# Attention's TensorE order in a fused pre-norm layer: score banks paired with halves of the row maxima, whole value products, and moved work at the edges of the stages

## The reference, cut to what matters

```python
x = L0_attn_x                                  # (4, 2048, 256), float32
x = x + attn(layernorm(x))                     # 16 heads of 16, causal
x = x + ffn(layernorm(x))

# attn:
qkv = x @ W_attn + b_attn
scores = einsum('bhqd,bhkd->bhqk', q, k) * 0.25
probs = softmax(where(causal, scores, -inf))
out = einsum('bhqk,bhkd->bhqd', probs, v) @ W_proj + b_proj

# ffn: ternary weights with one scale per row, a rank-16 term, squared ReLU
h = x @ (tern(w_fc) * scale).T + gate * (x @ v.T @ fast_b.T @ u.T)
y = (max(h, 0) ** 2) @ (tern(w_proj) * scale).T
```

## Time and profile before

| | |
|---|---|
| median of 3 runs | 2120.4 us (2115.23 to 2132.78) |
| profiled execution, its own time | 2129.81 us |
| its span, first to last instruction | 2128.1 us |
| QKV, span time | 0 to 189 us |
| opening, maxima alone | 189 to 237 us |
| attention's 16 units | 237 to 1724 us |
| MLP, first to last matmul | 1746 us to the end |
| PE busy | 2032.3 us, 96% |
| DVE busy | 1850.8 us, 87% |
| ACT busy | 1487.4 us, 70% |
| granted PE clock, mean | 0.967 |

### The profile page before, as it was taken

How to read it: one execution, slowest core, us unless ns; L and a number is a source line. 1 busy time by engine, 2 the same in 40 slices (tenths; PEclk the granted TensorE clock), 3 DMA queues, 4 the chain that set the end, 5 groups by cost and what they waited for, 6 DMA issues and landing times. The chain is left out here.

```text
span 2128.1 us, 46470 instructions
## 1 busy us (share of the span) xinstructions
PE 2032.3 (96%) x18173; PEld 1123.1 (53%) x18173; DVE 1850.8 (87%) x3143; ACT 1487.4 (70%) x2787; POOL 474.8 (22%) x637
## 2 busy tenths in 40 slices
PE   6987899999999999999999999999999969999998
PEld 5875344444444444444444444444444438888887
DVE  7987889999999999999999999999999438998996
ACT  2331378888888888888888888888888535555554
POOL 0000011011110111111011110111111127776774
PEclk9997599999999999999999999999999779999999
DMA  5995121221222212122121211212122122333220
GB/s 192 325 317 215 29 54 47 53 57 38 75 52 60 55 40 65 48 70 47 53 60 34 82 51 54 57 37 71 50 63 62 36 65 80 101 89 90 80 80 30
DMA packets 163003, 168.29 MB, mean 79 GB/s; under 512 B 74704, under 2 KB 102880, under 8 KB 162784
## 3 DMA queue, kind: packets, MB, share of 16 engines
q1 hardware_dynamic: 154112, 157.72, 25.4%
q10 hardware_dynamic: 8672, 7.60, 1.3%
HBM read 95.77 MB, written 67.63 MB: 77 GB/s over the span
## 5 line engine op out<-in xcount | busy, mean ns | idle before, releaser
L984 ACT ACTIVATE probs<-ps_s 128x512 f32<-128x512 f32 x2176 | 1179.3, 596 | 257.8 <-PE ps_s L1177 231.8
L1010 DVE TENSOR_REDUCE maxes<-ps_m 128x2 f32<-128x1024 f32 (+1 forms) x960 | 1141.9, 1220 | 110.5 <-PE ps_m L1140 88.4
L1198 PE MATMUL ps_acc<-probs,vs 128*32 128x256 f32 (+1 forms) x8696 | 703.9, 396 | 11.9 <-ACT acc_sb L962 11.9
L1177 PE MATMUL ps_s<-qs,ks 50*128 50x512 f32 (+3 forms) x2560 | 577.8, 450 | 1.0 <-ACT probs L984 0.9
L1140 PE MATMUL ps_m<-ks,qs 48*128 48x512 f32 (+3 forms) x2560 | 504.4, 392 | 18.7 <-DVE maxes L1010 9.5
L1177 PEld LDWEIGHTS ps_s<-qs,ks 50*128 50x128 f32 x2560 | 255.9, 186 | 414.0 <-ACT probs L984 381.1
L1198 PEld LDWEIGHTS ps_acc<-probs,vs 128*32 128x32 f32 x8696 | 173.7, 108 | 295.1 <-issue 194.7
L918 POOL TENSOR_SCALAR_AFFINE_SELECT probs<-probs 128x512 f32<-128x512 f32 x256 | 160.0, 640 | 744.1 <-ACT probs L984 740.5
L1140 PEld LDWEIGHTS ps_m<-ks,qs 48*128 48x128 f32 x2560 | 265.1, 192 | 94.5 <-DVE maxes L1010 70.7
L1017 DVE CUSTOM_DVE_ANT_0 sums_masked<-ps_m,mask 128x384 f32<-128x384 f32 (+1 forms) x512 | 186.6, 421 | 20.2 <-PE ps_m L1140 4.1
L1382 POOL TENSOR_TENSOR hid<-square,hid 128x512 fp32r<-128x512 f32 x128 | 175.3, 1378 | 107.3 <-DVE square L1393 91.9
(11 more groups left out here) (129 smaller groups left out, 1764.5 us busy)
## 6 DMA issues: line engine op xcount, KB each, us to landing
qs<-q_scr SPq DMA_DIRECT2D x384, 64.0 KB, 2.7
ks<-k_scr SPq DMA_DIRECT2D x384, 64.0 KB, 2.8
q_scr<-probs SPq DMA_DIRECT2D x32, 512.0 KB, 4.0
k_scr<-probs SPq DMA_DIRECT2D x32, 512.0 KB, 5.3
o_scr<-acc_sb SPq DMA_DIRECT2D x64, 256.0 KB, 2.9
v_scr<-probs SPq DMA_DIRECT2D x16, 512.0 KB, 5.8
v_dense<-v_scr SPq DMA_DIRECT2D x16, 512.0 KB, 4.5
o_in<-o_scr SPq DMA_DIRECT2D x32, 256.0 KB
```

The source lines that it names most:

```text
L984: act.activation(probs[:, s % RING, x], ps_s[:, k % BANKS], ACT.Exp).then_inc(ring_taken, 1)
L1010: last = dve.tensor_reduce(maxes[c % 2][:, :, pairs, tt, i], banks, AX.X, ALU.max)
L1177: last = pe.matmul(ps_s[:, k % BANKS, at:at + width], ks[u][rows, j // TT, p, j % TT * P:(j % TT + 1) * P], qs[u][rows, c, p, q0:q0 + widt ...
L1198: last = pe.matmul(ps_acc[h * VW:(h + 1) * VW, q0:q0 + width], vs[u][:, j, h], probs[:, s % RING, h % banks_of(s), at:at + width], start=( ...
```

## The change

In each step the order becomes bank 2i (r = 0), the r = 1 half of an item ("beside"), bank 2i+1 (r = 1), the r = 0 half of the item, for both pairs of banks, and then all value products of the step whole, 512 queries wide. The ring stays at three banks and the maxima at two slots.

At the edges: `fill` issues matmuls whose result nobody reads, behind each of the last ten items of the opening (3), in place of the values in the first three steps (4), and in six steps of the last unit (2). QKV's fixed loads go from ACT's to SP's queue, its first products stand ahead of the second transposes, and its last chunk is stored in the attention block. In the last unit PE's steps for the weights and the projection come earlier, chunk 1's attention output is loaded and scaled there, and the square root is taken ahead of the last copy of the accumulator. What the last accumulator still needs (store_acc, invert_sums, store_recip) moves into the MLP block, and ACT's high part of chunk 1 behind that of chunk 0.

```diff
 def order(s, last):
     x = sum(banks_of(i) // 2 for i in range(s))
-    if banks_of(s) == 4:
-        got = [("bank", 0), ("bank", 1), *items_at(x), ("values", (0,)), ("bank", 2), ("bank", 3), *items_at(x + 1), ("values", (1,))]
-    else:
-        got = [("bank", 0), ("bank", 1), ("values", (0, 1)), *items_at(x)]
+    got = []
+    for i in range(banks_of(s) // 2):
+        item, *others = items_at(x + i)
+        got += [("bank", 2 * i), ("beside", item[1]), ("bank", 2 * i + 1), item, *others]
+    got.append(("values", None))
...
-LOADS_AT, TERNARY_AT, O_AT, X_AT = 5, 16, 19, 22
-LOW_AT, G_AT, W1_AT, W2_AT, S_AT, PROJECT_AT = 17, 22, 25, 29, 33, 34
-SCALE_AT, BIAS_AT, O_HIGH_AT = 26, 30, 33
+LOADS_AT, TERNARY_AT, O_AT, X_AT, O1_AT = 5, 16, 20, 24, 32
+LOW_AT, G_AT, W1_AT, W2_AT, S_AT, PROJECT_AT = 16, 20, 21, 25, 29, 31
+SCALE_AT, BIAS_AT, O_HIGH_AT = 25, 29, 29
+FILLED_ITEMS, FILLED_STEPS = 10, (17, 18, 19, 32, 33, 34)
...
+def fill(pe, w_o, bank, count):
+    for _ in range(count):
+        pe.matmul(bank, w_o[:, 0, 0, 0:P], w_o[:, 0].rearrange("p k d -> p (k d)"), start=True, stop=True, skip_group_check=True)
...
@@ build_qkv, SP @@
+            sp.wait_ge(masked, 3)
...
+            sp.wait_ge(sh.ones_set, 1)
+            load_ones(sp, sh, sh.ks)
...
             def body(n, used, u, left):
+                if left > 0:
+                    store_chunk(sp, scr, sh, n)
@@ build_qkv, PE @@
-                if left >= 1:
+                if left >= 1 and n > 0:
                     transposes(n + 1, 1 - u)
...
                     last.then_inc(qk_ready, 1)
+                if n == 0:
+                    transposes(1, 1)
@@ build_attention, SP @@
+            store_chunk(sp, scr, sh, BATCH * NCH - 1)
...
-                if last:
-                    store_acc(n, NCH - 1)
-                    store_recip(n, NCH - 1)
+                    if last and s == O1_AT:
+                        sp.wait_ge(late.w2_ready, KH // 2)
+                        load_o(sp, scr, lead.o_in[1], lead.r_in[1], lead.o_loaded[1], 1)
@@ build_attention, ACT @@
                 if last:
+                    lead.norm.take_root(act, 0)
                     copy_acc(n, NCH - 1)
-                    lead.norm.take_root(act, 0)
@@ build_attention, PE @@
-            def form_max(n, par, k):
+            def form_max(n, par, k, r):
...
-                if not (isinstance(n, int) and NM * n + k < SLOTS):
+                if r == 1 and NM * n + k >= SLOTS:
                     pe.wait_ge(slot_freed, NM * n + k - SLOTS + 1)
...
-                last.then_inc(slot_filled, 1)
+                if r == 0:
+                    last.then_inc(slot_filled, 1)
...
                 if what == "item":
-                    form_max(0, 0, x[1])
+                    form_max(0, 0, x[1], 1)
+                    form_max(0, 0, x[1], 0)
+                    if x[1] >= LEAD - FILLED_ITEMS:
+                        fill(pe, keep["w_o"], ps_acc[:], 3)
...
+                        elif what in ("beside", "item"):
+                            form_max(*unit_of(x, n, u), 1 if what == "beside" else 0)
...
+                        elif what == "values":
+                            fill(pe, keep["w_o"], ps_acc[:], 4)
+                    if last and s in FILLED_STEPS:
+                        fill(pe, keep["w_o"], ps_m[:, 3], 2)
@@ build_mlp, SP, POOL, ACT @@
-            load(1)
+            load_x(sp, io, x[1], x_loaded[1], 1)
+            store_acc(sp, scr, lead, UNITS - 1, NCH - 1)
...
-            scale(1)
             bias(1)
...
-            act.wait_ge(o_ready, 2)
-            copy_high(act, o_t, o_in[1], o_scaled, o_copied, KD)
             for n in range(CHUNKS):
                 copy_high(act, xn_t, ps_t, turned, turned_copied, KD * n)
+                if n == 0:
+                    act.wait_ge(o_ready, 2)
+                    copy_high(act, o_t, o_in[1], o_scaled, o_copied, KD)
```

More of the change, by code:

```diff
@@ L125, in order @@
     x = sum(banks_of(i) // 2 for i in range(s))
-    if banks_of(s) == 4:
-        got = [("bank", 0), ("bank", 1), *items_at(x), ("values", (0,)), ("bank", 2), ("bank", 3), *items_at(x + 1), ("values", (1,))]
-    else:
-        got = [("bank", 0), ("bank", 1), ("values", (0, 1)), *items_at(x)]
[L130 to L139, removed]
+    got = []
[3 more added lines that the diff above has]
+    got.append(("values", None))
+    return [(what, y) for what, y in got if not (last and what in ("beside", "item", "found", "rows") and y[0])]
 def ring_uses(s, last):
@@ L656, in _ @@
             copy_high(act, xn_t[0], ps_t, xt_ready, xt_copied, 0)
-            act.wait_ge(masked, 3)
-            for r in range(2):
-                for half in range(2):
-                    for dst, src in ((sh.ident_half, keep["ident_h"]), (sh.mask_half, keep["mask_h"])):
-                        act.dma_start(dst[ROW * r:ROW * (r + 1), half], src[ROW * half:ROW * (half + 1), :]).then_inc(sh.fixed_in, 16)
-            act.wait_ge(sh.ones_set, 1)
-            load_ones(act, sh, sh.ks)
             norm.take_root(act, 1)
@@ L1115, in body @@
                         take_w2()
+                    if last and s == PROJECT_AT:
+                        copy_low(dve, lead.o_t, lead.o_in[0], lead.o_copied, lead.o_split, 0)
+                        for i in range(2):
+                            residual(dve, lead, lead.x, lead.x1, 0, i)
+                        lead.norm.variance(dve, 0)
                 if last:
-                    copy_low(dve, lead.o_t, lead.o_in, lead.o_copied, lead.o_split, 0)
-                    for i in range(2):
-                        residual(dve, lead, lead.x, lead.x1, 0, i)
-                    lead.norm.variance(dve, 0)
                     lead.norm.normalise(dve, lead.x1, lead.xn, 0).then_inc(lead.xn_ready, 1)
-                    invert(n, NCH - 1)
             over_units(dve, body)
@@ L1199, in values @@
                                          probs[:, s % RING, h % banks_of(s), at:at + width],
-                                         start=(j == 0 and 0 in halves), stop=(s + 1 in CHUNK_END), skip_group_check=True)
-                if 1 in halves:
-                    last.then_inc(pv_done, 1)
+                                         start=(j == 0), stop=(s + 1 in CHUNK_END), skip_group_check=True)
+                last.then_inc(pv_done, 1)
             def turn_low(n):
@@ L1237, in turn_scales @@
             def turn_scales():
+                pe.wait_ge(late.rows_made, 1)
                 pe.wait_ge(late.w2_taken, 3)
```

167 lines of the change are left out of this document (89 added, 78 removed).

## The result

The changed kernel took a median of 2195.9 us (2188.9 to 2198.6, four runs), the kernel before 2126.6 us (2115.2 to 2136.1, four runs) on the same chip: 1.032 times the time (95% interval 1.028 to 1.036). The forecast of 2138 had the sign right and the size wrong by 58 us, and the result lies outside the stated range of 2085 to 2168.

The account below looks back on a forecast made before the run. PE was taken to bound most of the kernel, with the bank ring's limit hidden behind it. Full steps +50, last unit -1, opening -8.5, QKV -6, way to MLP -18: +17 on 2120.4 gave 2138 us, range 2085 to 2168.

Parts of the forecast that it names:

- Part 1, full steps: Attention steps: a full step goes from 2.47 to 2.58 us; +3.3 a unit, +50 for 15 units.
- The ring: Three score banks: bank 3 waits for bank 0's exp, a loop of 1.24 us where three slots give only 1.0.
- a slot of 0.34: Full steps: the values follow bank 3's start by 0.34 us, in the sum 1.24 + 0.34 + 1.00 = 2.58.
- the slots: Steps with masked items in a row: an item's first half waits for its maxima slot; 0.5 us a unit, bounded by 1.2.
- Part 2, last unit: Last unit of attention: longer steps and fills against a held clock, sum -1 us (-4 to +11).
- the fills and the denser work would hold the clock: Last unit: TensorE's clock stays at 1.00 in steps with form_w1 and step 24, giving 11 us back.
- the clock falls in attention: Rival: waits in each step drop the clock to 0.50, costing 28 us per 85 us stretch; 2166 us, chance 0.10.
- Part 3, opening: Opening and first unit: fills raise the clock early; -8.5 us (-11 to +9).
- three items: Opening: the clock stays at 0.50 for only three items with fills, costing +2.5 us.
- the fills don't do what they are for: Rival: clock stays 0.50 through the opening and falls in the last unit; 2149 to 2165 us, chance 0.18.
- Part 4, QKV: QKV block: earlier end without the last chunk's store and earlier first products; -6 us (-9 to -2).
- Part 5: Attention to MLP: a copy's wait goes (-14), the root moves ahead, PE keeps its clock (3 less); -18 us (-20 to -13).

Follow-up runs that it names:

- kernel 3: Changed kernel with the new pairs kept but the values cut in halves, one behind each pair of banks; 2103.8 us, ratio 0.990.
- experiment 4: Changed kernel with both heads of an item together behind each pair of banks, values whole at the end; 2279.7 us, one execution.
- kernel 5: Changed kernel with exps over 256 of 512 columns in all units but the first; 2106.2 us, one execution.
- kernel 10: Changed kernel with exps over 64 of 512 columns in all units but the first and reductions over half the keys; 2005.3 us, one execution.
- kernel 6: Changed kernel with plain reductions over half of each item's keys; 2160.2 us, one execution.
- kernel 9: kernel 3 with one opening burst of sixteen fills, and chunk 1's x loaded and its bias added in the last unit; 2102.1 us, ratio 0.992.
- kernel 11: kernel 9 without the twelve fills of the last unit; 2100.1 us, ratio 0.991.
- kernel 7: kernel 3 without any fills in the opening and the first unit; 2103.4 us, ratio 0.991.
- kernel 12: Changed kernel with the old step order and halved values, exps over 64 columns except in the first unit, half-length reductions; 2089.7 us, one execution.

## Why the prediction was wrong

**Part 1, full steps: right mechanism, undersized.** The ring, its loop of 1.24 and the direction stood in the forecast and in the trace, and experiments 3, 4 and 5 show them from three sides. For the fifteen units I said +50; it was 59.8 for fourteen, and one more at 4.27 makes 64. Two terms were too small. I read the starts of the first exps of each step and took medians over the steady units, before and after:

```
steps of a unit                                       before    after   sum of differences   forecast
22 full steps, of which 19 at 2.66 to 2.68 after   2.46-2.72  2.66-2.80      +3.2              +2.35
5 steps where masked items stand in a row          2.79-2.99  3.16-3.50      +1.9              +1.05
5 others of four banks (two plain, three short)    2.43-2.67  2.39-2.73      -0.3              -0.1
4 steps of two banks                               1.67-2.07  1.59-1.88      -0.5               0
```

The first term is the stretch from bank 3 to the values. This is the step of the sum that failed: the prediction took a slot of 0.34; it is 0.43 after the wait, in kernel 10 without a long wait too, and 0.32 in kernel 3, where the values follow the second pair. I think of the weights of the values, whose load lies open there; no run separates it. The 0.09 on a full step is the difference between 2.58 and 2.67. The second is the slots: not 0.5 but up to 1.9 a unit, of which kernel 6 removes only 0.8 (in two of the five steps). What holds the other three, 17, 24 and 27 of a unit counted from 0, with half-length reductions as well, stays open; kernel 3 still has 17 and 24 at 3.13 and 3.14, so in these two it is mostly not the place of the values. Against this, two-bank steps gained 0.5, which I had put at nothing.

**Part 2, last unit: -1 forecast, +13.7 measured.** The step that failed is that the fills and the denser work would hold the clock, worth 11. In the changed kernel it fell three times, for 3.4 us at 1718.9, 23.9 at 1746.2 and 3.4 at 1783.7. PE's timeline after, steps with form_w1, and the same kind of step in kernel 3:

```profile
1744.70 0.73 PE L1202 MATMUL ps_s<-qs,ks 50*128 50x512 f32 x3
1745.94 0.61 PE L1202 MATMUL ps_s<-qs,ks 50*128 50x512 f32 x1 [0.51 <-ACT probs L1014]
...
1751.50 1.22 PE L1202 MATMUL ps_s<-qs,ks 50*128 50x512 f32 x3
...
1759.63 1.22 PE L1202 MATMUL ps_s<-qs,ks 50*128 50x512 f32 x3
```
```profile
1670.53 0.51 PE L1214 MATMUL ps_s<-qs,ks 50*128 50x512 f32 x2
...
1674.91 0.51 PE L1214 MATMUL ps_s<-qs,ks 50*128 50x512 f32 x2
```

4.4 us a step at 1.00 in kernel 3; 4.8 at 1.00 and up to 8.1 at 0.50 in the kernel after. Without maxima only three score matmuls fill the 1.24, so PE idles in each of these steps, 0.51 us at 1.00 and 0.32 at 0.50. A step without extra work takes 2.67 where kernel 3 takes 2.24, and one with form_w2 3.25 in place of 2.83: +0.43, where I had +0.34. The sizes come apart with kernel 3, whose last unit takes 100.7. Before to kernel 3 is -8.2, and my fills and clock together were +2.5 - 11 = -8.5; that they agree is luck in part, since the twelve fills cost 3.9 (kernels 9 and 11). Kernel 3 to after is +22. Four steps around the long fall take 25.3 us, where the same kinds of step at 1.00 take 16.1, which is 9; the two steps with the short falls take 5.3 and 7.2 us in place of 3.3 and 5.3, which is 3 beyond the ring's 0.43 each. That leaves some 10 for the ring, against a forecast of 7.5.

The rival "the clock falls in attention" thus came true in one place, the last unit, and not in the steady units, where PE idles 6% and the clock is 1.00 from 258 to 1719. The Trainium skill's page "TensorE: Matmul & The Clock Gate" (Part 1, the second failure mode) says that short idles between groups through PSUM banks let the clock oscillate. The traces agree in the last unit (idles of 0.51 us and a fall; no wait for an exp and no fall in kernels 3 and 10) and differ in the steady ones (idles of 0.27 in each step and no fall in 1402 us); kernel 7's short fall had no idle ahead of it.

**Part 3, opening: -8.5 forecast, +6 measured** (10.6 less 4.3 for the ring in unit 0). The step that failed is "three items": in this execution the clock stayed low for all ten. PE's timeline in the opening after:

```profile
222.03 1.65 PE L288 MATMUL ps_acc<-w_o 128*128 128x512 f32 x3
223.60 0.79 PE L1165 MATMUL ps_m<-ks,qs 48*128 48x512 f32 x2
224.33 1.65 PE L288 MATMUL ps_acc<-w_o 128*128 128x512 f32 x3
```

An item takes 2.30 us with its fills (224.33 - 222.03), 1.13 without, and all ten are paid at this price since the clock stayed 0.50 until 258.0. First reduction to first exp grew by 13.9 instead of 2.5. Nor did the fills fit beside DVE at 1.00, where I had put an item at 0.97 us: in kernel 5 it took 227.32 - 225.99 = 1.33. How late the clock rose differs between executions of the same code: in kernel 5 two items were paid at the low clock. Even there the two stretches gained only 1.9 us against before (149.2 against 151.1), or some 6 with unit 0's ring of 4.3 taken out, so that -8.5 was nearly reached; the +6 is the lot of the profiled execution of the changed kernel. The 12 that the clock is worth in unit 0 were right: unit 0 takes 90.7 in kernel 3 where the clock is 1.00 from its start, and 102.0 in kernel 7 where it is not. The rival "the fills don't do what they are for" named this: it put the opening and the first unit 16 above the forecast's -8.5, and they came out 15 above it, with a dearer opening and part of the gain in unit 0.

**Part 4, QKV: -6 forecast, -4.9 measured.** Right within its range; the first products start at 14.45 in place of 23.6, and little of this arrives, as argued.

**Part 5: -18 forecast, -10.4 measured.** The gap shrank by 16.1, as forecast, with 3.3 us from the last transposes to MLP's first matmul (1806.01 to 1809.35):

```profile
1806.01 1.07 PE L347 MATMUL ps_m<-ident,mxn 128*128 128x128 f32 x8 [2.97 <-DVE mxn L473]
...
1809.35 0.80 PE L168 MATMUL ps_s<-mxn_t,w 128*128 128x512 f32 x1 [2.27 <-DVE mxn_t L488]
```

The other term has the wrong sign: MLP's first chunk takes 5.7 more, not 3 less. The step that failed is that PE, idle for less time, would keep its clock. The shorter gap still holds two waits of PE, of 2.97 and 2.27 us (rows above), and the clock was at 0.50 from 1807.6 to 1814.4 and again from 1831.5 to 1838.3. The group of the second layer's first half among PE's matmuls of that chunk (count, busy, mean ns, idle before), in the kernel before and after:

```profile
L1467 PE MATMUL ps_s<-w,hid 128*128 128x256 f32 x32 | 4.2, 284 | 0.4 <-POOL hid L1382 0.4
```
```profile
L1501 PE MATMUL ps_s<-w,hid 128*128 128x256 f32 x32 | 7.1, 358 | 1.9 <-POOL hid L1414 1.8
```

With the other half (5.4 us in place of 4.2) the second layer's matmuls took 12.5 us in place of 8.4, since the clock fell again in the chunk (0.81 on average from 1809 to 1842), and PE waited 1.4 us more for POOL's product. The clock is not all: in kernel 3 it was at 0.50 for 3.4 us of the chunk, less than the 5.7 before, and the chunk still took 30.5 us. The 16 us of PE's idle time before were not all loss: other engines used them for work that now stands beside MLP's first matmuls. This last sentence is argued; kernel 9 removed only one candidate (x), and which of the others makes POOL late stays open.

## What to carry to other kernels

With a ring of n banks, compare what stands between bank k and bank k + n on the matmul engine with the loop from matmul through reader and back (here 1.24 us), before anything is merged or moved. An order that saves 0.17 us of matmul time can cost 0.37 of waiting, because the long piece that covered the loop has left its place; keep the long pieces spread, one between each pair of uses. Work issued only to raise the clock has to be costed at the low clock, for every instance: here small groups paid back what they took and no more, and what a solid burst brought was too small to show in the medians. Where the clock is involved, one profiled execution isn't enough: the same opening and first unit took 149 us in one and 162 in another.

## What was not expected of the hardware

- A pair of 512-column matmuls in different row groups can follow another at 0.24 us in place of 0.33: in kernel 10 the pairs start at 1002.47, 1002.81, 1003.05 and 1003.34. The first distance, right behind values, is the long one. The new pairing isn't what makes the short one: the kernel before has it too, where a third pair follows (pairs at 999.66, 1000.00 and 1000.23).
- In one execution the clock did not rise in 36 us in which fills of 128 rows alternated with maxima and the first scores (PE busy 95% from 235 to 258), and in another of the same code it rose 3.9 us after the first fill. With a solid burst it rose after 3.1 to 4.3 us in all three kernels that have one.
- It can also fall with no idle time near. Kernel 7, in the last unit, the 20.6 us ahead of a fall of 3.4 us:

```profile
1650.00:1670.60 20.60, 20.60 (x155) 8.90 (x152) 16.25 (x26) 12.68 (x26) 2.49 (x4) 1.00 0.03 4
```

- And it can stay low with PE recorded busy all the time. Kernel 12, in the middle of attention, a wait of PE for keys that a transfer brings, and the window of 47 us behind it:

```profile
1015.03 0.50 PE L1195 MATMUL ps_m<-ks,qs 48*128 48x512 f32 x2 [1.26 <-DMA ks<-k_scr]
```
```profile
1016.00:1063.00 47.00, 47.00 (x283) 16.97 (x279) 15.91 (x37) 7.37 (x43) 2.28 (x5) 0.50 0.08 21
```

  It is one stretch in one execution. The clock fell at 1015.7, right behind this wait of 1.26 us; whether the wait started it, and what ended the stretch, no run shows.
